# Layer-norm statistics of a fused attention and expert kernel: first batch's plane sums on GpSimd, later totals, root and Newton steps spread over three slots and two engines, token copies issued behind the reciprocals

## The chip, the cores and the metric

The kernel runs on one core of one Trainium2 chip. The metric is the device time of one execution in microseconds (us). The kernel before takes 1373.47 us, the median of three runs from 1370.99 to 1375.1 us. "PE" is TensorE, "DVE" VectorE, "ACT" ScalarE, "POOL" GpSimd and "SP" the engine that here only issues DMAs.

## The reference, cut to what matters

The input is an image x of shape 4 x 64 x 128 x 128 (batch, channel, height, width). It goes through window attention and then through an expert layer, each with a normalisation in front and a residual around it. The change touches the first normalisation, over the 64 channels of each pixel (and the order of two DMAs):

```
def _ln_c(v, eps=1e-06):
    m = jnp.mean(v, axis=1, keepdims=True)
    s = jnp.var(v, axis=1, keepdims=True)
    return (v - m) / jnp.sqrt(s + eps)
...
x = x + _L0_conv_ref(_ln_c(x), ...)      # 8x8 windows, 4 heads, softmax
t = _to_tokens(x)
t = t + _L0_ffn_ref(_ln_t(t), ...)       # router over 8 experts, the best two
```

So for each batch the kernel needs, at each of 128 x 128 pixels, the sum and the sum of squares over 64 planes, and from them the mean and one over the standard deviation.

## The kernel before

The image is turned in groups of four planes. PE transposes a group from `x_in` into a PSUM bank, ACT copies it to `xt` (width on the partitions, height along the row), and ACT squares it into `x_sq`. Two groups make a pair. `x_in` has four places (`RING`), so a load waits until the transposes of the group four before it are done (`x_turned`).

**The prologue.** The first batch has no earlier work to hide behind. A loop of four turns takes two pairs each. DVE sums each pair twice, the planes (`sum_planes`, L799) and the squares (`sum_squares`, L807). After the loop DVE adds up the totals (L820, L825), makes the variance in four small steps (`variances`), ACT takes the root (L625), and DVE takes its reciprocal and one Newton step in four small operations (`deviations`, result in `rstd`). GpSimd then multiplies mean and `rstd` (`scaled_means`, L1036) and normalises the first group (`normalise_input`, L1060, L1063), on which PE's first projection (L379) waits. Fourteen constants are loaded by SP between the first four groups of the image and the rest.

**The slots.** After that the work is a software pipeline of 64 strips of eight image rows, written out slot after slot. In slot j five stages are under way at once: project strip j+1, attend j, output j-1, route j-2 and mix j-3. Each engine's order in a slot is the order of the statements of its `slot` function, and engines meet only at semaphores. While a batch is worked on, the next batch is turned and summed in its slots: `planned(j)` says that slots 3 to 10 of a batch each take a pair (`take`), slots 4 to 11 sum one (`sums`), and slots 12, 13 and 14 do one step each, `SUM_UP`, `ROOT` and `MEANS`. This happens three times, for the batches after the first. In the slots it is already GpSimd that adds the planes (`add_planes`, L1050 and L1054).

**What stands around the steps.** At a slot's start DVE finishes the routing of the strip that is to be mixed, then waits for the small DMA `r_in` and takes the reciprocals of the softmax sums (`reciprocals`, L876). SP writes them to DRAM and reads them back spread over the partitions (`r_b`), which DVE's `normalise` (L882) uses in the middle of the slot. SP then issues the four copies of the routed tokens (`spread_tokens`, `t_t`), which the gates of the next slot read, then loads of the image, then the stores. ACT turns scores into probabilities by `exps` (L660). The functions of Sqrt and of Exp lie in different tables, so each change costs an ACT_TABLE_LOAD. GpSimd subtracts the maxima ahead of the exponentials (`shift`, L1069), multiplies two of the eight gates (L1091) and centres and scales the tokens.

## Time and profile before

| what | value |
|---|---|
| median of three runs | 1373.47 us |
| the profiled execution: its own time | 1371.55 us |
| its span, first to last instruction | 1369.8 us |
| mean granted TensorE clock | 0.985 |
| PE, DVE, ACT, POOL busy | 1246.1, 1162.3, 880.8, 882.2 us |
| PE, DVE, ACT, POOL share of the span | 91%, 85%, 64%, 64% |

The page gives the busy time of each engine over the whole span. That is an average over a prologue of some 50 us in which PE mostly waits, and over slots in which it hardly does, so the shares have to be read again by stage: the rows below do that by windows of single slots and by the timeline of the prologue. A slot is measured from one L876 on DVE to the next, since each slot has exactly one.

### The profile page before, as it was taken

To read this page: it belongs to the slowest core of one execution; us is meant where nothing else is said; L and a number is where in the kernel's file an instruction comes from. 1 tells how busy PE (TensorE), PEld (TensorE's weight loads), DVE (VectorE), ACT (ScalarE), POOL (GpSimd) and SP (SyncE) were. 2 spreads that over 40 slices of the span, in tenths; PEclk is the share of its full clock that TensorE was granted. 3 is DMA by queue.
4 is the path that set the end of the run, shared out by engine and by line. 5 is a ranking of instruction groups with operands and counts; after the bars stand their busy time and mean duration, and the time that the engine had idled before them with its cause. 6 is when DMAs were issued, how large, how long until landed. Compare 5 with 4: busy or idle time off the path is not lost.

```text
span 1369.8 us, 47545 instructions
## 1 busy us (share of the span) xinstructions
PE 1246.1 (91%) x19840; PEld 785.7 (57%) x19840; DVE 1162.3 (85%) x2476; ACT 880.8 (64%) x1617; POOL 882.2 (64%) x758
## 2 busy tenths in 40 slices
PE   4378999988999999998999999999899999999986
PEld 3266666555666656655555666665566656666542
DVE  7737889988888898998898899899888888888874
ACT  5356767766666767766666777775666666666632
POOL 0245777865766777785667678776666676766632
PEclk9989999999999999999999999999999999999998
DMA  6002423321222333332122333432222222222221
GB/s 179 16 11 65 96 65 89 89 63 36 66 66 46 92 88 75 79 72 65 42 59 64 75 80 87 95 67 49 64 54 55 61 62 65 55 53 65 58 65 39
DMA packets 95552, 91.52 MB, mean 67 GB/s; under 512 B 26797, under 2 KB 62253, under 8 KB 95342
## 3 DMA queue, kind: packets, MB, share of 16 engines
q1 hardware_dynamic: 95342, 88.49, 27.9%
q8 instruction: 159, 2.61, 0.8%
q14 instruction: 51, 0.42, 0.1%
HBM read 36.03 MB, written 17.83 MB: 39 GB/s over the span
## 4 chain that ended last, share of the span: by engine, by line
PE 55%; DVE 21%; ACT 9%; issue 7%; DMA 5%; POOL 1%; SPq 1%; DVEq 0%; POOLq 0%; ACTq 0%
PE bank_y L521 12%; PE bank_s L405 8%; PE bank_s L379 6%; DVE t_g L977 6%; PE bank_t L420 5%; PE bank_o L433 4%; PE bank_p L448 4%; PE bank_e L477 3%; ACT k_m L640 3%; DVE mx L869 3%; DVE x L891 3%; PE bank_o L460 2%; PE bank_g L510 2%; DMA r_b<-recip_rows 2%; PE bank_p L510 2%
## 5 line engine op out<-in xcount | busy, mean ns | idle before, releaser
L1069 POOL TENSOR_TENSOR prob<-prob,mx 128x512 f32<-128x512 f32 x256 | 261.5, 1043 | 92.4 <-DVE mx L869 92.2
L521 PE MATMUL bank_y<-t_g,w_exp 128*64 128x512 f32 x1024 | 281.5, 626 | 18.7 <-DVE t_g L977 13.7
L1091 POOL TENSOR_TENSOR t_g<-t_t,g_copy 128x512 f32<-128x512 f32 x128 | 165.6, 1293 | 151.5 <-ACT g_copy L692 151.2
L660 ACT ACTIVATE prob<-prob 128x512 f32<-128x512 f32 x256 | 160.8, 628 | 150.3 <-POOL prob L1069 148.7
L664 ACT ACTIVATE prob_t<-bank_t 128x512 f32<-128x512 f32 x256 | 152.3, 595 | 139.9 <-PE bank_t L420 139.7
L1081 POOL TENSOR_TENSOR ln<-ln,mhalf 128x8 f32<-128x8 f32 x64 | 105.0, 1640 | 158.2 <-DVE ln L905 158.2
L420 PEld LDWEIGHTS bank_t<-idn,prob 128*128 128x128 f32 x1024 | 111.2, 144 | 137.4 <-issue 103.5
L862 DVE TENSOR_TENSOR prob<-bank_s,rel 128x1024 f32<-128x1024 f32 x128 | 156.6, 1223 | 36.2 <-PE bank_s L405 31.1
L420 PE MATMUL bank_t<-idn,prob 128*128 128x128 f32 x1024 | 169.5, 289 | 17.6 <-ACT prob_t L664 10.4
L977 DVE TENSOR_TENSOR t_g<-t_t,bank_p 128x512 f32<-128x512 f32 x256 | 174.2, 680 | 6.0 <-PE bank_p L510 5.9
L405 PEld LDWEIGHTS bank_s<-k_m,q_t 32*64 32x64 f32 x4096 | 114.5, 135 | 72.2 <-issue 68.8
L869 DVE TENSOR_REDUCE mx<-prob 128x16 f32<-128x1024 f32 x128 | 151.9, 1187 | 0.1
L405 PE MATMUL bank_s<-k_m,q_t 32*64 32x128 f32 x4096 | 146.0, 280 | 1.9 <-ACT q_t L635 1.5
L379 PE MATMUL bank_s<-xn,w_qkv 64*64 64x128 f32 x3072 | 118.5, 284 | 23.8 <-POOL xn L1063 17.7
L640 ACT ACTIVATE k_m<-bank_s,k_bias,k_mask 128x512 f32<-128x512 f32 x128 | 99.1, 775 | 39.1 <-PE bank_s L379 39.1
L379 PEld LDWEIGHTS bank_s<-xn,w_qkv 64*64 64x64 f32 x3072 | 85.7, 136 | 57.2 <-issue 57.0
L521 PEld LDWEIGHTS bank_y<-t_g,w_exp 128*64 128x64 f32 x1024 | 53.4, 136 | 109.2 <-issue 101.9
L977 DVE TENSOR_TENSOR t_g<-t_t,bank_g 128x512 f32<-128x512 f32 x128 | 87.7, 685 | 20.0 <-PE bank_g L510 15.7
L510 PE MATMUL bank_g<-g_t,gate_sel 128*128 128x512 bf16 x256 | 98.5, 385 | 5.6 <-DVE t_g L977 5.6
L510 PE MATMUL bank_p<-g_t,gate_sel 128*128 128x512 bf16 x256 | 99.2, 388 | 2.0 <-DVE t_g L977 2.0
L692 ACT ACTIVATE g_copy<-bank_g 128x512 f32<-128x512 f32 x128 | 76.2, 595 | 20.3 <-PE bank_g L510 20.3
L1060 POOL TENSOR_TENSOR xn<-xt,rstd 128x512 f32<-128x512 f32 x64 | 81.8, 1278 | 10.2 <-PE bank_s L379 9.1
(111 smaller groups left out, 2398.2 us busy)
## 6 DMA issues: line engine op xcount, KB each, us to landing
t_t<-t_rout SPq DMA_DIRECT2D x256, 128.0 KB, 3.7
x_in<-in_x SPq DMA_DIRECT2D x68, 256.0 KB, 3.8
r_b<-recip_rows SPq DMA_DIRECT2D x64, 256.0 KB
out_y<-y_out SPq DMA_DIRECT2D x128, 128.0 KB, 2.5
r_in<-sum_b SPq DMA_DIRECT2D x64, 16.0 KB
recip_rows<-r_out SPq DMA_DIRECT2D x64, 16.0 KB, 1.4
gate_sel<-in_sel SPq DMA_DIRECT2D x1, 512.0 KB
rel<-in_relb SPq DMA_DIRECT2D x1, 256.0 KB
```

Of the source, the lines that this page charges most:

```text
L379: last = mm(dst[:, n], w_qkv[rows, i, :], src[:, n, ab], start=True, stop=True, skip_group_check=True)
L405: last = mm(S_S[C * b:C * b + C, hp, i, :, n, :], q_t[rows, p, w, :], k_m[rows, p, w, :, :], start=True, stop=True, skip_group_check=True)
L420: last = tr(B_T[:, h * P:(h + 1) * P], prob[:, i, h].rearrange("p n k -> p (n k)"), idn[:, :])
L510: mm(B_GATE[u % 2][:, :], gate_sel16[:, u, :], g_t[:, :], start=True, stop=True).then_inc(gate_done.sem, 1)
L521: mm(B_Y[C * a:C * a + C, :], w_exp[:, pair, :], t_g[:, (2 * pair + a) % TG, :], start=False, stop=(pair == MIXES // 2 - 1), skip_group_ch ...
L660: A(prob[:, i], prob[:, i], ACT.Exp).then_inc(p_ready.sem, 1)
L664: A(prob_t[:, i].rearrange("p h q -> p (h q)"), B_T[:, :], ACT.Copy).then_inc(pt_ready.sem, 1)
L862: V.tensor_tensor(prob[:, 2 * pair:2 * pair + 2].rearrange("p i (g e) n k -> p g i (e n k)", e=2), B_S[:, :, :].rearrange("p g (i s) -> p ...
L869: V.tensor_reduce(mx[:, 2 * pair:2 * pair + 2, :].rearrange("p i s -> p (i s)"), prob[:, 2 * pair:2 * pair + 2].rearrange("p i h n k -> p ...
L977: V.tensor_tensor(t_g[:, u % TG, :], t_t[:, p, u % 2, :], B_GATE[u % 2][:, :], ALU.mult).then_inc(tg_dve.sem, 1)
L1069: G.tensor_tensor(sc, sc, mx[:, i, :].unsqueeze(2).broadcast_to([P, 2 * HEADS, NTOK]), ALU.subtract).then_inc(s_shifted.sem, 1)
L1091: G.tensor_tensor(t_g[:, u % TG, :], t_t[:, p, u % 2, :], g_copy[:, n % 2, :], ALU.mult).then_inc(tg_pool.sem, 1)
```

## The change

- In the prologue GpSimd adds the planes with the same `add_planes` that it used for the later batches. DVE keeps only the squares. The squares go to two buffers in turn (`FIRST_SQ`, the second one laid over `prob`), and the loop of four turns is written out.
- The step `SUM_UP` of slot 12 and `ROOT` of slot 13 are taken apart. Slot 12 (`SQUARES`): DVE's total of the squares. Slot 13 (`PLANES`): DVE's total of the planes, then the variance on GpSimd (five operations) and the root on ACT. Slot 14 (`SCALES`): DVE's reciprocal, then the Newton step (four operations) and the scaled mean on GpSimd. The prologue uses the same functions one behind the other.
- DVE's three pieces stand ahead of `reciprocals` in the slot. In slot 13 GpSimd's variance stands behind `normalise_input`, and ACT's root ahead of the exponentials of the next strip. In slot 14 GpSimd's work stands ahead of the last two `shift`s.
- In the prologue ACT takes a root of a piece of the identity first, and the real root comes ahead of the constants' wait.
- SP issues the constants after the loads of the first batch, and issues the token copies only when the reciprocals' spread (`recip_spread`) has landed.

```
-            with eng.Fori(0, 4) as t:
+            for t in range(GROUPS // RING):
                 for r in range(2):
                     take(0, t, r)
...
                 if routing_on:
+                    if outputting:
+                        sp.wait_ge(recip_spread.sem, recip_spread.at(j - 1, 16))
                     spread_tokens(j - 2, p)
...
+            for t in range(1, GROUPS // RING):
                 load(t * RING, 0, RING)
+            for dst, src in consts:
+                sp.dma_start(dst[tuple(slice(None) for _ in dst.shape)], src).then_inc(loads, 16)
...
             def first_root(batch):
+                act.wait_ge(idn_loaded, 16)
+                A(rs[:, 1, 0:1], idn[:, 0:1], ACT.Sqrt).then_inc(set_act.sem, 1)
+                root(batch)
                 act.wait_ge(loads, ALL_LOADED)
...
-                if work.step == ROOT:
-                    root(work.batch)
                 if attending:
                     exps(j, 2)
...
+                if work.step == PLANES:
+                    root(work.batch)
                 if projecting:
                     exps(j + 1, 0)
...
                     routing(j - 3, 15, 19)
+                if work.step == SQUARES:
+                    total_squares(work.batch)
+                if work.step == PLANES:
+                    total_planes(work.batch)
+                if work.step == SCALES:
+                    turn_root(work.batch)
                 if outputting:
                     reciprocals(j - 1)
                 if attending:
                     maxima(j, 1)
-                if work.step == SUM_UP:
-                    total_sums(work.batch)
...
-                if work.step == SUM_UP:
-                    variances(work.batch)
-                if work.step == ROOT:
-                    deviations(work.batch)
...
+            def variances(batch):
+
+                pool.wait_ge(totals.sem, totals.at(batch, 2))
+                G.tensor_scalar(st[:, 2, :], st[:, 0, :], 1.0 / C, None, ALU.mult).then_inc(variance.sem, 1)
+                pool.wait_ge(variance.sem, variance.at(batch, 1))
+                G.tensor_tensor(st[:, 3, :], st[:, 2, :], st[:, 0, :], ALU.mult).then_inc(variance.sem, 1)
+                pool.wait_ge(variance.sem, variance.at(batch, 2))
+                G.tensor_tensor(st[:, 3, :], st[:, 1, :], st[:, 3, :], ALU.subtract).then_inc(variance.sem, 1)
+                pool.wait_ge(variance.sem, variance.at(batch, 3))
+                G.tensor_scalar(st[:, 4, :], st[:, 3, :], 0.0, 1.0 / C, ALU.max, ALU.mult).then_inc(variance.sem, 1)
+                pool.wait_ge(variance.sem, variance.at(batch, 4))
+                G.tensor_scalar(st[:, 4, :], st[:, 4, :], LN_C_EPS, None, ALU.add).then_inc(variance.sem, 1)
...
                 if routing_on:
                     scale_tokens(j - 2)
+                if work.step == SCALES:
+                    deviations(work.batch)
+                    scaled_means(work.batch)
                 if attending:
                     shift(j, 2)
                     shift(j, 3)
...
-                if work.step == MEANS:
-                    scaled_means(work.batch)
                 if projecting and not (isinstance(j, int) and j == LAST - 1):
                     normalise_input(j + 2)
+                if work.step == PLANES:
+                    variances(work.batch)
                 if mixing:
                     gate(j - 3, 1 - p, 6)
```

The first place is GpSimd's queue in the prologue. Before, its first operation on data is the scaled mean:

```order
L1036 TENSOR_TENSOR m_rstd<-st,rstd 128x128 [waits rstd_ready]
L1060 TENSOR_TENSOR xn<-xt,rstd 128x512 [waits mr_ready,qkv_done]
L1063 TENSOR_TENSOR xn<-xn,m_rstd 128x512 [waits xn_ready]
L1060 TENSOR_TENSOR xn<-xt,rstd 128x512 [waits qkv_done]
L1063 TENSOR_TENSOR xn<-xn,m_rstd 128x512 [waits xn_ready]
```

After the change 15 additions of planes come first (the last two are shown), then the variance (L1009 to L1017), the Newton step (L1024 to L1030) and the scaled mean:

```order
L1054 TENSOR_TENSOR plane_sum<-plane_sum,xt 128x512 [waits planes_added,xt_ready]
L1054 TENSOR_TENSOR plane_sum<-plane_sum,xt 128x512 [waits planes_added]
L1009 TENSOR_SCALAR st<-st 128x128 [waits totals]
L1011 TENSOR_TENSOR st<-st 128x128 [waits variance]
L1013 TENSOR_TENSOR st<-st 128x128 [waits variance]
L1015 TENSOR_SCALAR st<-st 128x128 [waits variance]
L1017 TENSOR_SCALAR st<-st 128x128 [waits variance]
L1024 TENSOR_TENSOR st<-st,rstd 128x128 [waits root_turned]
L1026 TENSOR_TENSOR st<-st,rstd 128x128 [waits newton]
L1028 TENSOR_SCALAR st<-st 128x128 [waits newton]
L1030 TENSOR_TENSOR rstd<-rstd,st 128x128 [waits newton]
L1035 TENSOR_TENSOR m_rstd<-st,rstd 128x128 [waits rstd_ready]
```

Each addition waits for the one before it, and every other one for a new pair of `xt`.

The second place is DVE's queue in slot 12 of a batch. Before, both totals stand between the maxima and the first gates (L977), and the variance behind these:

```order
L970 TENSOR_TENSOR g<-bank_e,g 128x4x32 [waits route]
L876 RECIPROCAL r_out<-r_in 128x32 [waits sum_cut]
L869 TENSOR_REDUCE mx<-prob 128x16 [waits s_biased]
L823 TENSOR_REDUCE st<-plane_sum 128x128 [waits planes_added,sq_sums]
L825 TENSOR_REDUCE st<-sums 128x128
L977 TENSOR_TENSOR t_g<-t_t,bank_g 128x512 [waits y_done,t_spread,gate_done]
L977 TENSOR_TENSOR t_g<-t_t,bank_p 128x512 [waits y_done,gate_done]
L830 TENSOR_SCALAR st<-st 128x128 [waits stat]
L832 TENSOR_TENSOR st<-st 128x128 [waits stat]
L834 SCALAR_TENSOR_TENSOR st<-st 128x128 [waits stat]
L837 TENSOR_SCALAR st<-st 128x128 [waits stat]
```

After the change one total is left in this slot, ahead of the reciprocal (now L849). The total of the planes (L818) stands in the same place of slot 13, and the reciprocal of the root (L824) in that of slot 14:

```order
L943 TENSOR_TENSOR g<-bank_e,g 128x4x32 [waits route]
L813 TENSOR_REDUCE st<-sums 128x128 [waits sq_sums]
L849 RECIPROCAL r_out<-r_in 128x32 [waits sum_cut]
L842 TENSOR_REDUCE mx<-prob 128x16 [waits s_biased]
L950 TENSOR_TENSOR t_g<-t_t,bank_g 128x512 [waits y_done,t_spread,gate_done]
L950 TENSOR_TENSOR t_g<-t_t,bank_p 128x512 [waits y_done,gate_done]
```

The third place is slots 13 and 14 on GpSimd. Before, the gates 2 and 6 (L1091) stand around the normalising of the next input, and only the scaled mean comes between (in slot 14):

```order
L1083 TENSOR_TENSOR t_n<-xc,ln 128x512 [waits lrstd]
L1069 TENSOR_TENSOR prob<-prob,mx 128x512 [waits mx_ready] x2
L1091 TENSOR_TENSOR t_g<-t_t,g_copy 128x512 [waits y_done,t_spread,g_copied]
L1036 TENSOR_TENSOR m_rstd<-st,rstd 128x128 [waits rstd_ready]
L1060 TENSOR_TENSOR xn<-xt,rstd 128x512 [waits mr_ready,qkv_done]
L1063 TENSOR_TENSOR xn<-xn,m_rstd 128x512 [waits xn_ready]
L1091 TENSOR_TENSOR t_g<-t_t,g_copy 128x512 [waits y_done,g_copied]
```

After the change, from the normalising of slot 13 on to its gate 6 (the five of the variance stand between them):

```order
L1063 TENSOR_TENSOR xn<-xn,m_rstd 128x512 [waits xn_ready]
L1009 TENSOR_SCALAR st<-st 128x128 [waits totals]
L1011 TENSOR_TENSOR st<-st 128x128 [waits variance]
L1013 TENSOR_TENSOR st<-st 128x128 [waits variance]
L1015 TENSOR_SCALAR st<-st 128x128 [waits variance]
L1017 TENSOR_SCALAR st<-st 128x128 [waits variance]
L1091 TENSOR_TENSOR t_g<-t_t,g_copy 128x512 [waits y_done,g_copied]
```

and at the start of slot 14, between the scaled tokens (L1083) and the shifts (L1069):

```order
L1083 TENSOR_TENSOR t_n<-xc,ln 128x512 [waits lrstd]
L1024 TENSOR_TENSOR st<-st,rstd 128x128 [waits root_turned]
L1026 TENSOR_TENSOR st<-st,rstd 128x128 [waits newton]
L1028 TENSOR_SCALAR st<-st 128x128 [waits newton]
L1030 TENSOR_TENSOR rstd<-rstd,st 128x128 [waits newton]
L1035 TENSOR_TENSOR m_rstd<-st,rstd 128x128 [waits rstd_ready]
L1069 TENSOR_TENSOR prob<-prob,mx 128x512 [waits mr_ready,mx_ready]
```

ACT's queue in slot 13, after the change, at the end of which the exponential of the next strip stands. The first table load carries no wait, the root behind it does:

```order
L696 ACTIVATE g_copy<-bank_g 128x512 [waits gate_done]
L627 ACT_TABLE_LOAD
L627 ACTIVATE st<-st 128x128 [waits variance]
L664 ACT_TABLE_LOAD
L664 ACTIVATE prob<-prob 128x512 [waits s_shifted]
```

Before, the same three rows (L625, L625, L660) stand in the first half of the slot, ahead of the exponential of the strip that is being attended.

## Rows read from the trace of the kernel before

**Rows 1.** The page, busy time by engine: us, share of the span, instructions.

```profile
PE 1246.1 (91%) x19840; PEld 785.7 (57%) x19840; DVE 1162.3 (85%) x2476; ACT 880.8 (64%) x1617; POOL 882.2 (64%) x758
```

**Rows 2.** Windows: length, then PE, PEld, DVE, ACT, POOL busy, granted clock, DMA.

```profile
301.30:323.50 22.20, 19.63 (x304) 11.68 (x303) 20.25 (x43) 12.20 (x23) 12.54 (x11) 0.92 0.23 51
323.50:345.40 21.90, 18.63 (x308) 11.63 (x308) 18.36 (x43) 15.30 (x27) 12.86 (x12) 1.00 0.23 52
345.40:364.40 19.00, 18.55 (x310) 11.79 (x309) 16.56 (x38) 12.66 (x25) 13.54 (x13) 1.00 0.26 59
1173.10:1191.90 18.80, 18.34 (x308) 11.63 (x308) 16.55 (x38) 12.50 (x24) 12.89 (x12) 1.00 0.26 60
```

**Rows 3.** Timeline of the prologue: start, duration, engine, line, operation [idle before].

```profile
10.34 0.60 ACT L607 ACTIVATE xt<-bank_s 128x512 f32 x1 [0.22 <-PE bank_s L357]
...
17.48 0.60 ACT L607 ACTIVATE xt<-bank_t 128x512 f32 x1
...
20.96 1.12 PE L357 MATMUL bank_t<-idn,x_in 128*128 128x128 f32 x4 [0.86 <-ACT xt L607]
...
41.56 1.22 DVE L820 TENSOR_REDUCE st<-sums 128x128 f32<-128x1024 f32 x1
...
45.16 1.28 ACT L625 ACT_TABLE_LOAD   x1 [5.88 <-DVE st L837]
...
46.80 0.95 DVE L844 RECIPROCAL rstd<-st 128x128 f32<-128x128 f32 x1 [1.72 <-ACT st L625]
...
48.70 0.29 DVE L852 TENSOR_TENSOR rstd<-rstd,st 128x128 f32<-128x128 f32 x1
...
53.17 1.98 PE L379 MATMUL bank_s<-xn,w_qkv 64*64 64x128 f32 x32 [17.71 <-POOL xn L1063]
```

**Rows 4.** Instructions by line, shapes apart: busy us, mean ns | idle before.

```profile
L1054 POOL TENSOR_TENSOR plane_sum<-plane_sum,xt 128x512 f32<-128x512 f32 x42 | 53.7, 1279 | 1.6
...
L807 DVE TENSOR_REDUCE sums<-x_sq 128x1024 f32 x8 | 15.2, 1898 | 0.0
```

**Rows 5.** Small GpSimd operations: by tile (ns min/median/max), and the memset of 128x128.

```profile
L1036 POOL TENSOR_TENSOR m_rstd<-st,rstd x4: 452/460/967, 49.1 to 989.3; 128x128 f32<-128x128 f32 x4
...
L1030 POOL MEMSET mhalf<- 128x128 f32 x1 | 0.2, 204 | 0.3 <-POOLq L1197 0.3
```

**Rows 6.** Timeline of DVE in slots 12 and 13.

```profile
301.30 0.35 DVE L876 RECIPROCAL r_out<-r_in 128x32 f32<-128x32 f32 x1 [1.54 <-DMA r_in<-sum_b]
...
302.65 1.03 DVE L823 TENSOR_REDUCE st<-plane_sum 128x128 f32<-128x512 f32 x1
...
323.50 0.35 DVE L876 RECIPROCAL r_out<-r_in 128x32 f32<-128x32 f32 x1 [0.93 <-DMA r_in<-sum_b]
...
327.95 0.95 DVE L844 RECIPROCAL rstd<-st 128x128 f32<-128x128 f32 x1 [1.60 <-ACT st L625]
```

**Rows 7.** Timeline of a slot without statistics, L876 at 364.35 and 382.92.

```profile
368.11 0.75 ACT L635 ACTIVATE q_t<-bank_s,q_bias 128x512 f32<-128x512 f32 x1
...
369.78 1.10 PE L405 MATMUL bank_s<-k_m,q_t 32*64 32x128 f32 x32
...
372.09 0.68 DVE L882 TENSOR_TENSOR o_t<-bank_o,r_b 128x512 f32<-128x512 f32 x1
...
373.01 0.59 ACT L692 ACTIVATE g_copy<-bank_g 128x512 f32<-128x512 f32 x1
...
373.68 1.30 POOL L1091 TENSOR_TENSOR t_g<-t_t,g_copy 128x512 f32<-128x512 f32 x1 [1.66 <-ACT g_copy L692]
...
376.01 0.63 ACT L660 ACTIVATE prob<-prob 128x512 f32<-128x512 f32 x1 [2.41 <-POOL prob L1069]
...
384.43 1.04 POOL L1069 TENSOR_TENSOR prob<-prob,mx 128x512 f32<-128x512 f32 x1 [1.12 <-DVE mx L869]
```

**Rows 8.** DVE's normalise by line, and the page's DMA issues of the tokens.

```profile
L882 DVE TENSOR_TENSOR o_t<-bank_o,r_b 128x512 f32<-128x512 f32 x64 | 43.7, 683 | 3.3 <-DMA r_b<-recip_rows 3.3
...
t_t<-t_rout SPq DMA_DIRECT2D x256, 128.0 KB, 3.7
```

More of the change, by code:

```diff
@@ L51 @@
 RING = 4
-SUM_UP, ROOT, MEANS = range(3)
+SQUARES, PLANES, SCALES = range(3)
 CHUNK = 32
@@ L281, in _ @@
                 sp.dma_start(x_in[:, r], xg[r]).then_inc(x_loaded[r].sem, 16)
-            for dst, src in consts:
-                sp.dma_start(dst[tuple(slice(None) for _ in dst.shape)], src).then_inc(loads, 16)
             def load(n, first, count):
@@ L839, in deviations @@
-            def deviations(batch):
-                r_std = rstd[:, bass.ds(batch % 2, 1), :].rearrange("p o h -> p (o h)")
-                root, half, v = (st[:, n, :] for n in (1, 3, 4))
-                dve.wait_ge(root_ready.sem, root_ready.at(batch, 1))
-                V.reciprocal(r_std, root).then_inc(newton.sem, 1)
-                dve.wait_ge(newton.sem, newton.at(batch, 1))
-                V.tensor_tensor(half, v, r_std, ALU.mult).then_inc(newton.sem, 1)
-                dve.wait_ge(newton.sem, newton.at(batch, 2))
-                V.tensor_tensor(half, half, r_std, ALU.mult).then_inc(newton.sem, 1)
-                dve.wait_ge(newton.sem, newton.at(batch, 3))
-                V.tensor_scalar(half, half, -0.5, 1.5, ALU.mult, ALU.add).then_inc(newton.sem, 1)
-                dve.wait_ge(newton.sem, newton.at(batch, 4))
-                V.tensor_tensor(r_std, r_std, half, ALU.mult).then_inc(rstd_ready.sem, 1)
+                V.tensor_reduce(st[:, 1, :], sums2[:, :, :], AX.X, ALU.add).then_inc(totals.sem, 1)
@@ new lines, in total_planes, with turn_root @@
+            def total_planes(batch):
+                dve.wait_ge(planes_added.sem, planes_added.at(batch + 1))
+                V.tensor_reduce(st[:, 0, :], plane_sum[:, :, :].rearrange("p c h -> p h c"), AX.X,
+                                ALU.add).then_inc(totals.sem, 1)
+            def turn_root(batch):
+                dve.wait_ge(root_ready.sem, root_ready.at(batch, 1))
+                V.reciprocal(rstd[:, bass.ds(batch % 2, 1), :].rearrange("p o h -> p (o h)"), st[:, 1, :]
+                             ).then_inc(root_turned.sem, 1)
@@ L1048, in add_planes @@
                 if done < 0:
-                    pool.wait_ge(stat.sem, stat.at(batch - 1, 1))
+                    if batch:
+                        pool.wait_ge(totals.sem, totals.at(batch - 1, 2))
                     G.tensor_tensor(plane_sum[:, :, :], halves[0], halves[1], ALU.add).then_inc(planes_added.sem, 1)
@@ L1052, in add_planes @@
                 for k in range(2):
[L1053 removed]
+                    pool.wait_ge(planes_added.sem, planes_added.at(batch, done + k))
                     G.tensor_tensor(plane_sum[:, :, :], plane_sum[:, :, :], halves[k], ALU.add).then_inc(planes_added.sem, 1)
@@ L1117, in first_means @@
             def first_means(batch):
+                variances(batch)
+                deviations(batch)
                 scaled_means(batch)
                 normalise_input(0)
-            pipeline(pool, slot, lambda batch, t, r: None, lambda batch: None, first_means)
+            pipeline(pool, slot, add_planes, lambda batch: None, first_means)
 SET_DVE = 14 + 2 + 3 * PARTS - 1
```

77 lines of the change are left out of this document (30 added, 47 removed).

## Prediction

> **What bounds the kernel now.** I read the page first: PE is busy for 91% of the span and DVE for 85% [rows 1]. That average hides two regimes, so I cut the span into windows. A slot that does no statistics takes 18.8 us with PE busy for 18.34 of them, so PE's own instructions fill it [rows 2]. In slots 12 and 13 of a batch, where the statistics are finished, the windows are 22.2 and 21.9 us long and PE is busy for 19.63 and 18.63: these slots are longer because PE waits. In the first of them the granted clock is 0.92, so part of PE's busy time there is slow work and not more work. Slot 14 takes 19.0. Against three slots of 18.8 that is 6.7 us too much for each batch, and 20.1 for the three batches that are summed in slots. This is all that the steps' spreading can give.
>
> The second regime is the prologue. PE starts its first projection at 53.17, after 17.71 us of idling that ended with the normalised input [rows 3]. Nothing else runs there, so each microsecond off that chain comes off the total until another chain takes its place.
>
> **The prologue, part by part.** The loop before is set by DVE, which reduces each pair twice at 1.9 us (1.90 for the squares [rows 4]; the planes have the same size). The last pair is done when the totals begin, at 41.56 [rows 3]. The change takes the planes off DVE, which leaves 8 x 1.9 us, and asks what is late next.
>
> - Transposes and copies. A turn of the loop that nothing holds up goes from ACT's copy at 17.48 to the next turn's transposes at 20.96, done at 22.08: 4.6 us [rows 3]. The second pair was ready at 10.94 (10.34 + 0.60). Three more turns put the last pair at 24.7.
> - GpSimd. It adds at 1.28 us with a gap of 1.6/42 = 0.04 [rows 4], and 14 of its 15 additions come after 10.94: 14 x 1.32 = 18.5, so it ends at 29.4. One turn asks 4 x 1.32 = 5.3 us of it, more than the 4.6, so GpSimd sets the loop now.
> - DVE. The last squares, 1.2 us of ACT behind the last pair, are reduced at 27.8 and totalled at 29.0 (1.22 like the row at 41.56). This hides behind GpSimd. The total of the planes then takes 29.4 + 1.03 [rows 6] = 30.4.
> - Variance on GpSimd. A two-input operation of 128x128 takes 0.46 there; a tensor_scalar is not in the trace. It has one input, so it lies between the memset's 0.20 and 0.46 [rows 5]; I take the middle, 0.33. With gaps of 0.06: 2 x 0.46 + 3 x 0.33 + 0.3 = 2.2, which gives 32.6.
> - Root and reciprocal. Before, the table load (1.28) began when the variance was ready and the root itself took from 46.44 to 46.80 [rows 3]. The dummy root now loads the table while GpSimd still adds, so only 0.36 is left: 33.0. The reciprocal, 0.95 and a gap: 34.0.
> - Newton step on GpSimd. 3 x 0.46 + 0.33 + 0.2 = 1.9. DVE prepares the weights at the same time, and the one m_rstd that ran beside that work took 0.97 where the others took 0.46 [rows 5]: 0.51 lost. Four operations could lose 0 to 2.0 us; I take 1.0, so `rstd` is ready at 36.9.
>
> Before it was ready at 48.99 (48.70 + 0.29), and what follows up to PE's 53.17 is unchanged, 4.2 us. **The prologue gives 12.1 us.** The constants now come after the loads, but their first users are the weights' preparation on DVE at 34 and PE at 41, so their delay costs nothing if they land by then; before, their 14 issues stood in front of the second set of loads. With tensor_scalar between 0.20 and 0.46 in the four places and the contention between nothing and 2.0, the gain is 10.7 to 13.5.
>
> The Trainium skill (GPSIMD Engine Reference, Specifications) says that GpSimd shares its SBUF interfaces with VectorE and contends with VectorE instructions that have two SBUF inputs or a two-port mode. The 0.97 agrees. By that rule the 14 additions would not suffer, since VectorE's reductions beside them have one input.
>
> **The slots, part by part.**
>
> - DVE's three pieces. Ahead of the reciprocal DVE sat idle for 1.54 us in slot 12 and 0.93 in slot 13, waiting for the DMA `r_in` [rows 6]. The total of the squares (1.22) fits into the first. The total of the planes (1.03) sticks out of the second by 0.1. The reciprocal (0.95) about fills the third. So 0.1 instead of 1.03 + 1.2 + four steps + 1.6 of waiting [rows 6] + five steps: this is where the 6.7 goes.
> - GpSimd in slot 13. `normalise_input` ends 1.66 us before gate 6 begins, since that waits for ACT's copy [rows 7]. The variance takes 2.2, so gate 6 and all behind it (the shifts of the next strip, its centred tokens, the squares on ACT and, through them, DVE's token variance and PE's turned tokens) come 0.55 later. I let that pass in full.
> - ACT in slot 13. The copy of gate 6 ends at 373.60 and the exponential starts at 376.01, 2.41 later [rows 7]. Table load, root and table load need 1.28 + 0.36 + 1.28 = 2.9 [rows 3]. As the first load carries no wait it starts at once, so the exponential starts at 376.5, within the 0.55 that the shift is late anyway. Nothing is added.
> - GpSimd in slot 14. The shift at the start of a slot follows an idle 1.12 [rows 7]. Ahead of it now stand the Newton step and the scaled mean, 1.9 + 0.46 + 0.1 = 2.5, so it comes 1.35 late. Queued behind it are the exponential, the copy for gate 2, and the queries `q_t`. ACT has `q_t` ready at 368.86 and PE reads it at 369.78, 0.92 later [rows 7]; the rest, 0.45, reaches PE.
>
> That is 0.1 + 0.55 + 0.45 = 1.1 us per batch against 6.7, a gain of 5.6, and **16.8 us for three batches**. If the slack of 0.92 does not hold and each operation is at its dear end, it is 0.1 + 1.0 + 2.0, a gain of 3.6 each or 10.8; if all hides, 20.1.
>
> The Trainium skill (ScalarE: Activation LUTs, What ACT_TABLE_LOAD costs) gives about 2.66 us for a switch of tables, load and drain together. In this trace the root's table load ended at 46.44 and the root was done and consumed by 46.80, so there is no such drain; with two switches of 2.66 and the root the exponential of slot 13 would be 3.2 late instead of 0.55, 8 us over the three batches.
>
> **The tokens.** DVE waited for `r_b` 3.3 us in all, in 64 normalisations [rows 8]. Issued behind it, the token copies no longer share its DMA time: 0 to 3.3 us, I take 1.0. The price would be tokens that are late for the next slot. `r_b` is there when DVE uses it, at 372.09; four issues and a landing of 3.7 [rows 8] from there end near 378.5, and the gate that reads them follows the slot's reciprocal at 382.92: over 4 us of slack. SP's loads and stores behind them slip by as much; the loads are for a slot later than the next.
>
> **The sum** is made against the profiled execution, 1371.55: 1371.55 - 12.1 - 16.8 - 1.0 = 1341.7. The median of the three runs lies 1.9 above that execution; I put the median of the changed kernel at 1343.
>
> **The rivals.** About 0.3%, 4 us, is what a measurement of this kernel can tell from no change.
>
> - *GpSimd passes its work on in full.* The variance and the Newton step with the mean each delay PE by their whole length, 2.2 + 2.5 + 0.1 = 4.8, and a batch gains only 1.9. For it speaks that PE has hardly any idle time in a plain slot, so any late input is felt; against it the idle times of 1.66 and 1.12 that stand ahead of GpSimd's work. It gives 1371.55 - 12.1 - 5.7 - 1 = 1352.8, a median of 1354.
> - *The image loads set the prologue.* Between 10.94 and 17.48 no pair was copied, while the constants stood ahead of the loads. Where a turn takes over 5.3 us the loads decide; at 7 us the last pair is there at 31.9, its additions end at 34.5 instead of 29.4, and 5.1 us are lost: 1348.
> - *All hides*, and `r_b` gives all it can: 1371.55 - 12.1 - 20.1 - 3.3 = 1336.
> - *The table switch costs what the page says*: 1351.
> - *Slower: late tokens.* The gates wait for copies that queue behind `r_b`, in each of some 61 slots. It decides once a slot grows by 30/61 = 0.5 us, and needs a landing over 4 us later than I have it. At 1 us a slot it gives 1343 + 61 = 1404. The slack speaks against it.
> - *No change*: both gains are eaten by new waits, for instance by tokens that are late by just that 0.5 us: 1372.
>
> **How the numbers follow.** My forecast has 0.52 (its own range 1338 to 1348), the full delay 0.19, the loads 0.12, all hidden 0.09, the table 0.02, late tokens 0.03, no change 0.03. The range of 1336 to 1355 leaves out the last two and the far ends of the first ones, some 2 in 10 in all. Faster by over 0.3%: 0.94; the same 0.03; slower 0.03.
>
> **What would show it.** In the profile after: PE's first projection near 41 us; GpSimd adding planes without a pause from 11 to 29 us; the tensor_scalars there at 0.2 to 0.46; slot 12 at 18.8, slots 13 and 14 at 19 to 19.6 us; the table loads in slot 13 directly behind gate 6's copy; `r_b` hardly waited for. The prediction is wrong if plain slots change their length, if slot 14 grows by 2 us or more, or if a wait for constants or for `t_t` appears.

## The result, and the profile after

The changed kernel takes 1341.52 us, the median of four runs (1339.54 to 1341.82), and the kernel before took 1372.9 beside it: a ratio of 0.9768, with an interval of 0.975 to 0.9786. The profiled execution spans 1340.0 us against 1369.8, so 29.8 us less. Among the executions of the kernels further down one, of the kernel with the new prologue alone, took 6206 us; it counts in the median given there and not in the ratio.

The page's busy times, against [rows 1]: GpSimd gains 36 us of work, DVE loses 24.

```profile
PE 1237.9 (92%) x19840; PEld 781.4 (58%) x19840; DVE 1138.4 (85%) x2436; ACT 875.7 (65%) x1615; POOL 918.0 (69%) x809
```

Windows of slots 12, 13 and 14 of the first batch summed in slots, and of a slot without statistics, with the columns of [rows 2]:

```profile
289.47:308.15 18.68, 18.21 (x307) 11.43 (x306) 17.48 (x39) 12.32 (x24) 12.76 (x12) 1.00 0.26 61
308.15:328.12 19.97, 18.59 (x310) 11.70 (x309) 17.42 (x40) 15.15 (x27) 15.30 (x17) 1.00 0.24 56
328.12:347.26 19.14, 18.13 (x305) 11.27 (x304) 16.50 (x38) 12.34 (x24) 15.12 (x17) 1.00 0.24 58
347.26:366.01 18.75, 18.32 (x307) 11.60 (x308) 16.56 (x37) 12.52 (x24) 12.83 (x12) 1.00 0.26 61
```

The slots of 22.20 and 21.90 are now 18.68 and 19.97. A slot is measured at L849, the reciprocals; in slot 14 that row has DVE's reciprocal of the root ahead of it, so below I also measure from one turning of the tokens on PE (L472) to the next, which gives 18.78, 20.15 and 18.96 for the three.

The prologue on GpSimd, a timeline, which answers to [rows 3]:

```profile
10.91 2.64 POOL L1054 TENSOR_TENSOR plane_sum<-plane_sum,xt 128x512 f32<-128x512 f32 x2 [0.97 <-ACT xt L609]
13.71 16.45 POOL L1054 TENSOR_TENSOR plane_sum<-plane_sum,xt 128x512 f32<-128x512 f32 x12 [0.17 <-ACT xt L609]
31.30 0.55 POOL L1009 TENSOR_SCALAR st<-st 128x128 f32<-128x128 f32 x1 [1.14 <-DVE st L818]
...
33.74 0.54 POOL L1017 TENSOR_SCALAR st<-st 128x128 f32<-128x128 f32 x1
35.69 0.90 POOL L1024 TENSOR_TENSOR st<-st,rstd 128x128 f32<-128x128 f32 x1 [1.41 <-DVE rstd L824]
```

and on ACT and PE:

```profile
25.61 1.28 ACT L631 ACT_TABLE_LOAD   x1
34.31 0.31 ACT L627 ACTIVATE st<-st 128x128 f32<-128x128 f32 x1 [7.20 <-POOL st L1017]
...
41.70 1.99 PE L381 MATMUL bank_s<-xn,w_qkv 64*64 64x128 f32 x32 [17.86 <-POOL xn L1063]
```

GpSimd adds almost without a pause until 30.16 (13.71 + 16.45), the table is loaded at 26.89, long before the root, and PE begins at 41.70 instead of 53.17.

Slot 13 on GpSimd and ACT:

```profile
315.99 0.55 POOL L1009 TENSOR_SCALAR st<-st 128x128 f32<-128x128 f32 x1
...
318.44 0.54 POOL L1017 TENSOR_SCALAR st<-st 128x128 f32<-128x128 f32 x1
319.05 1.29 POOL L1091 TENSOR_TENSOR t_g<-t_t,g_copy 128x512 f32<-128x512 f32 x1
```

```profile
317.63 1.28 ACT L627 ACT_TABLE_LOAD   x1
319.00 0.31 ACT L627 ACTIVATE st<-st 128x128 f32<-128x128 f32 x1
319.33 1.28 ACT L664 ACT_TABLE_LOAD   x1
321.37 0.63 ACT L664 ACTIVATE prob<-prob 128x512 f32<-128x512 f32 x1 [0.76 <-POOL prob L1069]
```

Gate 6 starts at 319.05 with no idle time ahead of it, where it had 1.66 [rows 7]. ACT was ready for the exponential at 320.61 and waited 0.76 more for GpSimd's shift. So the variance is what is late here, and the two table loads hide behind it.

In slot 14 the shift starts directly behind the scaled mean, 3.16 us after the slot's reciprocals at 328.12, where it is 1.51 in a slot without statistics [rows 7]; it is 1.65 late:

```profile
331.28 2.04 POOL L1069 TENSOR_TENSOR prob<-prob,mx 128x512 f32<-128x512 f32 x2 [0.18 <-POOL m_rstd L1035]
```

The rows that answer to [rows 8], DVE's normalise and the landing of the tokens:

```profile
L855 DVE TENSOR_TENSOR o_t<-bank_o,r_b 128x512 f32<-128x512 f32 x64 | 43.5, 680 | 0.0
...
t_t<-t_rout SPq DMA_DIRECT2D x256, 128.0 KB, 2.4
```

DVE waits for `r_b` no more, and the tokens land in 2.4 us instead of 3.7 (the last figure of the row).

Cut at the reciprocals, the 29.8 us are: 11.2 before the first of them (83.8 to 72.6), 16.5 in the nine slots with steps (189.7 to 173.2), 2.2 in 24 slots without any work for the next batch (454.1 to 451.9), and nothing beyond 0.5 in the 26 slots that take or sum image groups.

### The profile page after: what moved, and what is told of

Read it like the earlier page. It is cut to its first block, busy times and chain, and to the rows that moved or that the text cites. A ratio compares the mean times of both kernels' runs of the same rounds, so it can differ in the third digit from the quotient of the medians.

```text
span 1340.0 us, 47446 instructions
## 1 busy us (share of the span) xinstructions
PE 1237.9 (92%) x19840; PEld 781.4 (58%) x19840; DVE 1138.4 (85%) x2436; ACT 875.7 (65%) x1615; POOL 918.0 (69%) x809
## 4 chain that ended last, share of the span: by engine, by line
PE 50%; DVE 23%; ACT 10%; issue 8%; POOL 7%; DMA 1%; SPq 1%; POOLq 0%; DVEq 0%; ACTq 0%
PE bank_y L523 10%; PE bank_s L407 8%; PE bank_s L381 6%; DVE t_g L950 6%; PE bank_t L422 5%; PE bank_o L435 4%; DVE mx L842 4%; DVE x L864 4%; PE bank_p L450 3%; PE bank_e L479 3%; ACT k_m L644 3%; PE bank_g L512 2%; DVE o_t L855 2%; ACT prob_t L668 2%; PE bank_e L472 2%
## 5 line engine op out<-in xcount | busy, mean ns | idle before, releaser
L1069 POOL TENSOR_TENSOR prob<-prob,mx 128x512 f32<-128x512 f32 x256 | 261.7, 1044 | 88.5 <-DVE mx L842 87.8
L1091 POOL TENSOR_TENSOR t_g<-t_t,g_copy 128x512 f32<-128x512 f32 x128 | 165.4, 1292 | 125.5 <-ACT g_copy L696 125.2
L422 PE MATMUL bank_t<-idn,prob 128*128 128x128 f32 x1024 | 169.1, 288 | 12.7 <-ACT prob_t L668 10.6
```

The source lines that it names most:

```text
L422: last = tr(B_T[:, h * P:(h + 1) * P], prob[:, i, h].rearrange("p n k -> p (n k)"), idn[:, :])
L1069: G.tensor_tensor(sc, sc, mx[:, i, :].unsqueeze(2).broadcast_to([P, 2 * HEADS, NTOK]), ALU.subtract).then_inc(s_shifted.sem, 1)
L1091: G.tensor_tensor(t_g[:, u % TG, :], t_t[:, p, u % 2, :], g_copy[:, n % 2, :], ALU.mult).then_inc(tg_pool.sem, 1)
```

## The experiments

All ratios are against the kernel before on the same chip; its medians there were 1376.59 (the first four kernels below), 1377.57 (the next four) and 1376.89 (the last four). My theory was that the gain is a sum of three independent parts: a prologue that GpSimd's additions set, slots in which only GpSimd's lateness is left, and a small relief of `r_b`.

### The new prologue alone

The kernel after with the steps of slots 12 to 14 put back on DVE and the wait ahead of the tokens taken out. The edit is shown in short, with comments for where the pieces went; ACT's root and the scaled mean went back to their old places too:

```
                 if work.step == SQUARES:
-                    total_squares(work.batch)
+                    total_sums(work.batch)        # behind maxima, as before
+                    dve_variances(work.batch)     # behind the first gates, as before
...
                 if routing_on:
-                    if outputting:
-                        sp.wait_ge(recip_spread.sem, recip_spread.at(j - 1, 16))
                     spread_tokens(j - 2, p)
```

> The new prologue alone; the steps in slots 12 to 14 and the token copies as before. Theory of separate gains: PE's first projection at 41.7 us as in the changed kernel instead of 53.2, and everything behind it as before, so 1372.9 - 11.5 = 1361 us, with slots 12 and 13 again at 22.1 and 21.9 us. Rival, that part of the prologue's gain is given back when the slots begin (constants late, loads of the next batch late): 1364 us or more, with the first slots longer than before.

It took 1366.51, ratio 0.9918 (0.9904 to 0.9933), 11.3 us less. PE's first projection stands at 41.71, as in the full change, and the nine slots with steps take 191.1 us (189.7 in the kernel before). The part agrees with the 11.5 us by which the first projection moved, with no sign that some of it was given back; the rival's 1364 was set against a median of 1372.9, and here the kernel before takes 1376.59.

### The new slots alone

The prologue of before, the steps of after, no wait ahead of the tokens.

> The steps of slots 12 to 14 alone; prologue and token copies as before. Theory of separate gains: the three slots take 18.6, 20.0 and 19.1 us instead of 22.1, 21.9 and 19.2, three times, so 1372.9 - 16.5 = 1356 us. Rival, that the slots need the later token copies because DVE now reaches its normalising earlier and waits for r_b: a wait for r_b of some 1 us in each of the nine slots, 1360 us or more.

It took 1362.41, ratio 0.9901 (0.9886 to 0.9916), 13.6 us less, so 3 less than the theory expected. The nine slots with steps did shrink, to 175.1. What the theory did not have: DVE waited 9.0 us for `r_b` in this run, against 3.3 in [rows 8]. That is as much as the rival named, but not where it placed it: three of the nine slots with steps have 2.5 us of it together, and the rest falls in other slots.

### The tokens' wait alone, and all but the wait

The kernel before with only these lines added, and the kernel after with only these taken out:

```
                 if routing_on:
+                    if outputting:
+                        sp.wait_ge(recip_spread.sem, recip_spread.at(j - 1, 16))
                     spread_tokens(j - 2, p)
```

> The kernel before with one edit: the token copies wait until the reciprocals' spread has landed. Theory: the 3.3 us that DVE waits for r_b fall to 0 and the time falls by 0 to 3.3 us, 1370 to 1373, most likely 1371.5. Rival, late tokens: the gates of the next slot wait for t_t and the time rises by over 4 us, 1377 or more.

> The changed kernel without the wait ahead of the token copies. Theory of separate gains: 1341.5 + 1 to 2 = 1343 us, with DVE's wait for r_b back at some 3 us. Rival, that the wait for r_b has grown with the slots that became shorter: 1346 or more.

The wait alone took 1371.17, ratio 0.9956 (0.9939 to 0.9972): 6.1 us less, beyond the 3.3 that I had as the most. All but the wait took 1346.14, ratio 0.9791 (0.9773 to 0.9808), which is the rival's time and not the theory's 1343. DVE's normalise by line, first with the wait alone and then with all but the wait, shows why; the tokens land in 3.6 us in the second, in 2.4 in the first:

```profile
L884 DVE TENSOR_TENSOR o_t<-bank_o,r_b 128x512 f32<-128x512 f32 x64 | 43.6, 681 | 0.0
```

```profile
L853 DVE TENSOR_TENSOR o_t<-bank_o,r_b 128x512 f32<-128x512 f32 x64 | 43.7, 683 | 8.2 <-DMA r_b<-recip_rows 8.2
...
t_t<-t_rout SPq DMA_DIRECT2D x256, 128.0 KB, 3.6
```

The 8.2 us fall in 13 slots. One of them, first without the wait (DVE and SP), then the same slot of the changed kernel run again, SP's DMA issues:

```profile
658.71 0.35 DVE L847 RECIPROCAL r_out<-r_in 128x32 f32<-128x32 f32 x1 [0.95 <-DMA r_in<-sum_b]
...
667.92 0.69 DVE L853 TENSOR_TENSOR o_t<-bank_o,r_b 128x512 f32<-128x512 f32 x1 [1.19 <-DMA r_b<-recip_rows]
...
678.67 0.35 DVE L847 RECIPROCAL r_out<-r_in 128x32 f32<-128x32 f32 x1 [0.92 <-DMA r_in<-sum_b]
```

```profile
659.09 0.32 SPq L299 DMA_DIRECT2D recip_rows<-r_out  x1
662.66 0.62 SPq L301 DMA_DIRECT2D r_b<-recip_rows  x1
663.33 2.43 SPq L309 DMA_DIRECT2D t_t<-t_rout  x4
```

```profile
660.69 0.32 SPq L299 DMA_DIRECT2D recip_rows<-r_out  x1
663.86 0.63 SPq L301 DMA_DIRECT2D r_b<-recip_rows  x1
667.45 2.44 SPq L309 DMA_DIRECT2D t_t<-t_rout  x4
```

In both the write of `recip_rows` is slow here: `r_b` is issued 3.6 and 3.2 us after it, where 1.4 is the rule in some 40 of the 64 slots. With the tokens beside it `r_b` then takes 667.92 - 662.66 = 5.3 us, alone at most 667.45 - 663.86 = 3.6 (the tokens are issued once it has landed). The slot without the wait is 19.96 us long, the other 18.73: the 1.19 of waiting passed in full to the slot. In all, the 24 slots without work for the next batch took 458.4 us without the wait and 452.0 with it.

The record also shows when `r_b` comes late. The write takes over 2.5 us in 16 to 21 of the 64 slots in each of the seven traces compared (both profiles, the four kernels of parts and the changed kernel again), with the wait ahead of the tokens and without. In the four of them without the wait DVE waited for `r_b` 43 times, 39 of them in slots with a slow write (2.2 us or more), so it takes both, a slow write and the tokens beside `r_b`. The rival's reason, slots that became shorter, does not hold: the kernel with the new prologue alone has the slots of before and waited 7.0 us.

### The changed kernel again

> The changed kernel itself, on the same chip as the three behind it. If the token wait is worth more where DVE waits longer for r_b, its ratio to the kernel before is lower than the 0.9791 of the kernel without that wait by 0.003 to 0.005, 0.975 to 0.977, with no wait for r_b. If the token wait is worth next to nothing, 0.978 to 0.980.

It took 1342.24, ratio 0.9756 (0.974 to 0.9773), with 452.0 in the plain slots and 173.3 in the slots with steps. So the wait is worth 0.9791 - 0.9756 = 0.0035 here, the first of the two cases expected. The three parts multiply to 0.9918 x 0.9901 x 0.9956 = 0.9777, and the first two to 0.9820, where the kernel with both took 0.9791 (0.9773 to 0.9808). Taken together the parts thus give as much as their sum or a little more, up to some 4 us; with intervals of 2 us on each part these runs can't say whether that surplus is real.

### Is slot 13 GpSimd's or ACT's?

Two multiplications of 128x128 more behind the variance on GpSimd:

```
                 if work.step == PLANES:
                     variances(work.batch)
+                    for _ in range(2):
+                        G.tensor_tensor(mhalf_pad[:, :], mhalf[:, :], mhalf[:, :], ALU.mult).then_inc(padded.sem, 1)
+                        pads += 1
+                        pool.wait_ge(padded.sem, pads)
```

> The changed kernel with two more operations of 128x128 on GpSimd behind the variance in slot 13, some 1.05 us with their gaps, in three batches; their result is not used. Theory, that slot 13 is late by what GpSimd's variance is longer than the idle time ahead of gate 6: slot 13 grows from 20.0 to 20.9 to 21.1 us. Rival, that ACT's two table loads set slot 13: it stays at 20.0 to 20.2.

One execution, 1345.56. Slot 13 grew from 20.15 to 21.09 and 21.10 (from one turning of the tokens to the next): 0.94 of the 1.05 that was added. The same two loads of tables stand in both. GpSimd sets this slot; the rival, that the switch of tables does, falls.

### The variance in forms that are dear and cheap

```
-                G.tensor_scalar(st[:, 2, :], st[:, 0, :], 1.0 / C, None, ALU.mult)
+                G.tensor_scalar(st[:, 2, :], st[:, 0, :], 1.0 / C, 0.0, ALU.mult, ALU.add)
...
-                G.tensor_scalar(st[:, 4, :], st[:, 3, :], 0.0, 1.0 / C, ALU.max, ALU.mult)
+                G.tensor_scalar(st[:, 4, :], st[:, 3, :], 1.0 / C, LN_C_EPS, ALU.mult, ALU.add)
-                G.tensor_scalar(st[:, 4, :], st[:, 4, :], LN_C_EPS, None, ALU.add)
+                G.tensor_scalar(st[:, 4, :], st[:, 4, :], LN_C_EPS, None, ALU.max)
```

> The changed kernel with the three tensor_scalars of the variance in other forms (mult with add twice, one max alone; the same value but for rounding). In the trace of the changed kernel mult with add takes 0.30 us, the others 0.54 to 0.65. Theory: the variance takes 2.4 us instead of 3.0, PE's first projection comes 0.5 earlier, slot 13 falls from 20.0 to about 19.4, in all 2 us off the changed kernel. Rival, that the duration goes by position and not by form: each stays at 0.54 to 0.65 and nothing moves.

It took 1340.74, ratio 0.9741 (0.9724 to 0.9758). The tile `st` in the changed kernel and in this one (ns min/median/max):

```profile
L1009 POOL TENSOR_SCALAR st<-st x4: 551/552/552, 31.3 to 943.4; 128x128 f32<-128x128 f32 x4
...
L1015 POOL TENSOR_SCALAR st<-st x4: 647/649/650, 33.0 to 945.1; 128x128 f32<-128x128 f32 x4
L1017 POOL TENSOR_SCALAR st<-st x4: 536/536/539, 33.7 to 945.8; 128x128 f32<-128x128 f32 x4
```

```profile
L1009 POOL TENSOR_SCALAR st<-st x4: 297/298/299, 31.2 to 942.2; 128x128 f32<-128x128 f32 x4
L1015 POOL TENSOR_SCALAR st<-st x4: 297/298/299, 32.7 to 943.7; 128x128 f32<-128x128 f32 x4
L1017 POOL TENSOR_SCALAR st<-st x4: 531/532/532, 33.1 to 944.0; 128x128 f32<-128x128 f32 x4
```

A multiplication followed by an addition takes 0.30 us, a multiplication alone 0.55, a maximum followed by a multiplication 0.65, and a maximum alone (0.53) as much as an addition alone (0.54). The rival, that the place decides, falls: the first and the fourth operation changed with their form. Slot 13 fell to 19.54, by 0.61, which is what the two rows gave up (0.60). The step in time is within the intervals; the rows are what shows it.

### Four steps instead of three

The takes and sums begin one slot earlier, the variance moves to the end of GpSimd's slot 12, and the root alone is left in slot 13:

```
-            if 3 <= n <= 11:
+            if 2 <= n <= 10:
...
-            if n - 12 in (SQUARES, PLANES, SCALES):
-                return Work(batch, step=n - 12)
+            if n - 11 in (SQUARES, PLANES, ROOT, SCALES):
+                return Work(batch, step=n - 11)
```

> The changed kernel with takes and sums one slot earlier and four steps: squares in slot 11, planes in 12 with the variance at the very end of GpSimd's slot, root in 13, reciprocal and Newton step in 14. GpSimd is idle for 2.5 us at that place, the variance takes 3.0. Theory: slot 12 costs 0.4 to 0.5 us over a plain slot, slot 13 0.5 for the two table loads (2.9 in 2.4 of idle time), slot 14 0.35 as now, so the sum stays within 0.5 us of now and the time within 1 us of the changed kernel. Rival, that slot 13 now waits for nothing but GpSimd: without it the table loads hide and a batch gains 1 us, 3 us in all.

It took 1341.18, ratio 0.9745 (0.9729 to 0.9761), 1.1 us under the changed kernel, about as expected. The rival, 3 us less by hidden table loads, falls. With the variance gone slot 13 is 19.30 long, not 18.78, and ACT's timeline shows the table loads uncovered:

```profile
315.99 0.59 ACT L696 ACTIVATE g_copy<-bank_g 128x512 f32<-128x512 f32 x1
316.60 1.28 ACT L627 ACT_TABLE_LOAD   x1
317.89 0.31 ACT L627 ACTIVATE st<-st 128x128 f32<-128x128 f32 x1
318.22 1.28 ACT L664 ACT_TABLE_LOAD   x1
319.51 0.63 ACT L664 ACTIVATE prob<-prob 128x512 f32<-128x512 f32 x1
```

From the end of the copy to the exponential it is 2.93 us, against 2.41 in [rows 7]: 0.52 late, and the slot is 0.52 longer. Slot 12, which took the variance in, grew by 0.7 (19.48), more than the 0.4 to 0.5 expected, so the spreading moved most of its gain to the neighbour. The Trainium skill (ScalarE: Activation LUTs, What ACT_TABLE_LOAD costs) adds a drain of some 1.38 us to each load; here each load is followed within 0.01 us by the function, so no such drain shows.

### The constants in front of the loads again

> The changed kernel with the constants' loads back ahead of the image's fifth group. Theory: the third pair is copied some 4 us later (transposes at 14.9 instead of 11.0), GpSimd's last 12 additions follow from there without a pause, so they end 3.3 us later and PE's first projection comes at 45.0 instead of 41.6; the time rises by 3 to 4 us, ratio 0.978. Rival, that GpSimd, being the slower one, has caught nothing up and loses nothing because it is already behind: PE at 41.5 to 42.5, ratio 0.976.

It took 1346.53, ratio 0.9781 (0.9758 to 0.9804), the 0.978 of the theory. GpSimd's additions in the prologue:

```profile
17.74 16.48 POOL L1055 TENSOR_TENSOR plane_sum<-plane_sum,xt 128x512 f32<-128x512 f32 x12 [4.21 <-ACT xt L610]
```

The additions wait 4.21 us for the image instead of 0.17, and PE starts at 45.77 instead of 41.53. Moving the constants is thus worth 4.2 of the prologue's 11.5 us. The other 7.3 were not split further by a run.

### The last additions left out in the first batch

This kernel leaves out the planes of the last pair of the first batch (its means are those of 56 planes), so GpSimd ends two additions earlier.

> The changed kernel in which GpSimd leaves out the planes of the first batch's last pair (it adds two single columns instead of 2 x 512 elements, so the first batch's means are not the reference's). Theory, that GpSimd sets the prologue's loop: its additions end 2.4 us earlier, DVE's total of the planes then follows that of the squares at 28.8 instead of 30.2, and PE's first projection comes 1.4 us earlier, at 40.1 to 40.3. Rival, that ACT's copies or the loads set it: PE's first projection stays at 41.5.

One execution, 1341.7, with the first projection at 39.56: 1.97 less than in the run of the changed kernel again (41.53), and more than the 1.4 expected. GpSimd's end and DVE's total of the planes in it:

```profile
27.56 0.46 POOL L1050 TENSOR_TENSOR plane_sum<-plane_sum,xt 128x1 f32<-128x1 f32 x2
```

```profile
28.05 1.02 DVE L818 TENSOR_REDUCE st<-plane_sum 128x128 f32<-128x512 f32 x1
```

With the two small operations that stand in for the additions GpSimd ended at 28.02, 1.96 before the 29.98 of that other run, and the total of the planes followed it at once, so all of it passed on to PE. GpSimd sets the loop, and the rival falls. DVE's total of the squares ended at 27.90, so the squares are the next chain; how far it lies behind varies, since in the traces of the kernels that have the new prologue unchanged DVE waited 0.7 to 2.3 us for GpSimd here. The span, 1339.9 against 1340.5, gained only 0.6, which one execution can't tell from nothing: with PE's start within 0.2 us of 41.6, the first reciprocals of these kernels stand anywhere from 69.97 to 72.62.

### Tokens later still

The rival that ends slower, tried: the tokens wait until DVE has added the attention's output to `x`, late in the slot.

```
-                        sp.wait_ge(recip_spread.sem, recip_spread.at(j - 1, 16))
+                        sp.wait_ge(x2_ready.sem, x2_ready.at(j - 1, 1))
```

> The changed kernel in which the token copies wait for DVE's residual (x2_ready, some 11 us into the slot) instead of the reciprocals' spread (some 6 us). Theory, that the tokens have slack: issued at 11, landed at 16, wanted at 20, so the time stays within 2 us of the changed kernel, ratio 0.975 to 0.977. Rival, late tokens or a late store and r_in behind them on SP: plain slots longer than 18.8 us, ratio above 0.980.

It took 1359.1, ratio 0.9878 (0.9858 to 0.9897): some 17 us of the gain gone, where the theory had at most 2. The profiled execution is the fastest of the four (1353.75), so its trace shows 11.5 us of them. No gate waits for `t_t`, so the loss is not where the prediction's rival had placed it; the rival set down for this run had the right engine, the stores and `r_in` behind the tokens on SP, but in the plain slots. The plain slots are as before (452.9); the 26 slots that take image groups grew from 522.7 to 536.9. SP's issues in one of them, in this kernel and in the changed kernel again:

```profile
180.90 3.88 SPq L309 DMA_DIRECT2D t_t<-t_rout  x4
184.83 1.19 SPq L287 DMA_DIRECT2D x_in<-in_x  x2
186.06 1.16 SPq L317 DMA_DIRECT2D out_y<-y_out  x2
187.27 0.66 SPq L293 DMA_DIRECT2D r_in<-sum_b  x1
```

```profile
173.45 3.20 SPq L309 DMA_DIRECT2D t_t<-t_rout  x4
176.69 1.18 SPq L287 DMA_DIRECT2D x_in<-in_x  x2
184.32 1.13 SPq L317 DMA_DIRECT2D out_y<-y_out  x2
186.26 0.66 SPq L293 DMA_DIRECT2D r_in<-sum_b  x1
```

Four issues of tokens, two of loads and two of stores now stand back to back ahead of `r_in`, on which the next slot's reciprocals wait. In the changed kernel SP waited 6.4 us for the stores' data and 0.8 for the sums in this stretch, so it had 7.2 to spare; here the tokens begin 7.1 later, counted from the slot's reciprocals (168.50 here, 168.19 there), and their issues take 0.7 longer. So `r_in` is issued 0.7 later in the slot and then takes 2.5 us to the reciprocals instead of 2.0, beside the stores, and this slot is 21.23 long instead of 20.05. DVE's wait for it in the whole run, from the waits of this kernel:

```profile
DVE r_out L849 <- DMA r_in<-sum_b: 77.0, 55, 4.4
```

In the changed kernel it is 58.9 and, run again, 61.4.

### The two mends together

The cheap forms and the four steps.

> The four steps and the other forms together. Theory: the variance, 2.4 us, now fits into GpSimd's 2.5 idle us at the end of slot 12, which becomes a plain slot by PE's clock marks (18.8), slot 13 keeps 0.5 for the table loads and slot 14 0.2, so each batch takes 0.6 us less than with either edit alone; with the 0.5 of the prologue the time is 2.5 to 3 us under the changed kernel, ratio 0.973 to 0.974. Rival, that the earlier takes cost elsewhere what the steps save: no better than 0.9745.

It took 1338.27, ratio 0.9725 (0.9705 to 0.9744), the lowest median of all, though its interval overlaps those of either mend alone; slots 12, 13 and 14 are 18.84, 19.30 and 19.09, and PE starts at 40.77. With the variance at 2.4 us instead of 3.0, slot 12 hides it.

## Why the prediction was right, point by point

The forecast of 1343 is 1.5 above the median measured, and the sum itself, 1341.7 for the profiled execution, meets the 1341.82 that this execution took (with the 1.9 that the prediction adds for the median it would have been 1343.6 and not 1343, and the range of the prologue comes out as 10.6 to 13.6; neither changes anything). So close a hit is luck in part: the three terms held, 12.1, 16.8 and 1.0 forecast against 11.5, 16.5 and 2.2, with errors in opposite directions, and executions of one kernel lie 2 us and more apart.

- **The prologue**, 12.1 forecast, 11.5 measured. The chain is the one named: GpSimd's additions (29.4 forecast, 30.16 measured, since from one to the next it is 1.37 and not 1.32; each itself took 1.27, so beside DVE's reductions they were not slowed, as the prediction had it), total, variance, root, reciprocal, Newton step. The variance took 2.98 instead of 2.2. The Newton step took 2.4 instead of 2.9: only its first operation lost time to DVE (0.90, where the others of its kind took 0.45), and my 1.0 for contention was double. What follows it took 3.7 instead of 4.2, since the scaled mean takes 0.45 and not 0.97. The constants' place alone holds 4.2 of the 11.5. The sum never priced it apart: its turns of 4.6 us from 10.94 on suppose loads that come in time, and the rival of the image loads says what happens otherwise. Putting the constants back in front brought that rival about, 4.2 lost against the 5.1 it had.
- **The mis-sized price** is the tensor_scalar on GpSimd. I had bounded it by a memset below and a two-input operation above, 0.20 to 0.46; three of the four take 0.54 to 0.65. The reason given for the upper bound, "it has one input", was the wrong one: the form of the operation decides, not the number of inputs. The Trainium skill (GPSIMD Engine Reference, Engine selection) calls one-input work on GpSimd roughly line-rate and two-input work the slow kind; here the trace differs, since all forms but the multiply-then-add cost more (0.53 to 0.65) than a two-input operation of the same size (0.45).
- **The slots**, 5.6 a batch forecast, 5.5 measured (16.5 for three). Slot 12 became a plain slot. Slot 13 pays 1.37 and not 0.65, which puts it outside the 19 to 19.6 us that the prediction named as a sign, since the variance with its gaps fills 3.1 us and overruns the idle 1.66 by 1.5; the padded kernel and the one with cheap forms show that this passes on nearly one for one. Slot 14 pays 0.2 and not 0.45. The two errors have different signs, and the nine slots had 6.8 us a batch to give where the forecast's first batch had 6.7; that part of the agreement is luck.
- **The table loads** in slot 13 cost nothing, as forecast, but only because the variance covers them: alone they cost 0.52, which is the 2.9 against 2.41 that the prediction worked out.
- **The tokens**, 1.0 forecast, 2.2 measured in the plain slots of the first two profiles, and by the ratios on the other chips 6.1 us alone and 4.8 on top of the rest. The step that was too small is "DVE waited for `r_b` 3.3 us in all": it is one execution's. Without the wait three other executions waited 7.0, 9.0 and 8.2 us. The wait goes with the slow writes of `recip_rows`: over 3 us in 8 slots of the kernel before, in 12, 18 and 12 of those three. Why the write is slow in some slots is open.
- **The late tokens.** The slack of "over 4 us" was right for the gates, which did not wait with 7.1 us of delay either, and wrong for SP. What is next behind the tokens is the next slot's `r_in`, and in a slot with image loads SP has 7.2 us to spare, which the delay of 7.1 and the 0.7 of longer issues overran.
- **Full delay by GpSimd** was half true: nearly full in slot 13, beyond the idle 1.66 (1.37 of 1.5), and not in slot 14, where the shift came 1.65 late (1.35 forecast) and PE 0.2: the 0.92 of slack in the queries took part of it, and what took the rest no run shows.

## What to carry to other kernels

Price an operation that moves to another engine by its exact form, since two forms of the same work can differ by a factor of two on one engine, and check whether the move fits in the idle time that stands ahead of the next operation there. What overruns it may pass on nearly in full, as in slot 13, or be taken up by slack further on, as in slot 14, so follow it to the engine that bounds the stage. When a wait is added to an engine that only issues DMAs, follow its queue to the first issue of the next stage, not only to the readers of what was delayed. A small broadcast that an engine waits for should not share its flight with bulk copies that have slack.

## What the runs showed of the hardware

- GpSimd, 128x128 f32: 0.30 us for multiply-then-add, 0.55 for multiply alone, 0.54 for add alone, 0.53 for maximum alone, 0.65 for maximum-then-multiply, 0.45 for a two-input operation.
- The 0.90 of the Newton step's first operation and the 0.97 of the old scaled mean both lie beside DVE's cast of `gate_sel`. Beside DVE's two-input additions of `b_exp` the next operation on GpSimd kept its 0.45, and it was DVE's that took longer, 0.56 instead of 0.29. The prediction counts the 0.97 as agreeing with the contention rule that it cites; the cast has one input, so this holds only if it works in the two-port mode, which no row shows.
- The granted TensorE clock in a window can't be trusted at the start of a trace. Windows of the kernel before, and then of the kernel after, with the columns of [rows 2]:

```profile
35.00:55.00 20.00, 2.29 (x35) 1.67 (x33) 17.73 (x28) 4.07 (x8) 3.49 (x3) 1.00 0.09 26
```

```profile
25.00:45.00 20.00, 1.99 (x32) 1.61 (x32) 14.62 (x24) 3.67 (x8) 12.58 (x16) 0.54 0.38 109
```

Both hold a first projection of 32 matmuls that takes 1.98 and 1.99 us, where later ones take 1.10 (79.89 us before, 68.88 after), yet one window reads 1.00, the level of 2.4 GHz, and the other 0.54, near that of 1.2 GHz. The trace's list of clock changes settles it: its first entry stands at 74.6 us in the kernel before and at 19.8 us in the kernel after, both to the full level, and ahead of it a window reads 1.00 whatever the matmuls do. From there on the two agree. In the kernel after, a group's four transposes take 1.06 to 1.09 us up to 19 us and 0.63 to 0.66 from 20.61 on; the level falls at 26.6, PE having been idle since 23.8, and projections take 1.98 at 54.75 (0.50) and 1.10 at 68.88 (1.00). In the kernel before they take 1.99 at 66.16 and 1.10 at 79.89. So the durations say that PE ran at half pace there until after 66 us, for all that the column reads 1.00, and the mean clocks of the two profiles, 0.985 and 0.975, can't be compared. In the prologue I therefore went by durations and not by this column.
